# A six-layer local-attention transformer stage: clamp of the norms, layer norm's rows and the order of three steps changed

## The reference

```python
DIM, DEPTH, HEADS, DIM_HEAD, WINDOW = 128, 6, 16, 64, 32
DIM_INNER = int(DIM * 4 * 2 / 3)                         # 341
def l2norm(t):
    return t / jnp.maximum(jnp.linalg.norm(t, axis=-1, keepdims=True), 1e-12)
def attn_layer(x, Wqkv, qs, ksc, Wo):
    q, k, v = split of x @ Wqkv into 16 heads of 64
    q = rotary(l2norm(q) * qs); k = rotary(l2norm(k) * ksc)
    sim = q k^T * 8, masked to this and the previous window of 32
    return softmax(sim) v @ Wo
def ffn_layer(x, g, bln, W1, b1, W2, b2):
    mu = x.mean(-1, keepdims=True)
    var = ((x - mu) ** 2).mean(-1, keepdims=True)
    xn = (x - mu) / jnp.sqrt(var + 1e-05) * g + bln
    a, gate = jnp.split(xn @ W1 + b1, 2, -1)
    return a * jax.nn.gelu(gate, approximate=False) @ W2 + b2
for i in range(DEPTH):
    x = attn_layer(shift_tokens(x), ...) + x
    x = ffn_layer(shift_tokens(x), ...) + x
```

## Time and profile before

| | us |
|---|---|
| median of 3 runs | 6615.09 |
| lowest and highest | 6614.57, 6616.69 |
| the profiled execution's time | 6612.73 |
| its span on the core | 6610.9 |

### The profile page before, as it was taken

How to read it: one execution, slowest core, us unless ns; L and a number is a source line. 1 busy time by engine, 2 the same in 40 slices (tenths; PEclk the granted TensorE clock), 3 DMA queues, 4 the chain that set the end, 5 groups by cost and what they waited for, 6 DMA issues and landing times. The chain is left out here.

```text
span 6610.9 us, 172137 instructions
## 1 busy us (share of the span) xinstructions
PE 5118.0 (77%) x73958; PEld 3242.9 (49%) x74006; DVE 4022.1 (61%) x5250; ACT 3052.2 (46%) x4513; POOL 2655.6 (40%) x1366
## 2 busy tenths in 40 slices
PE   4749999999999999999999994888896444444446
PEld 3326666666666666666666662544543222122234
DVE  3167777777777777777877773233333544444554
ACT  1225555555555555555555552333333333343245
POOL 0025555555555555555555551111011444434400
PEclk9669999999999999999999996788887777777778
DMA  0010001001000100100010000000000000000000
GB/s 21 0 39 15 17 16 37 16 18 27 26 15 18 30 22 17 28 23 18 17 32 19 18 17 9 3 2 2 2 1 7 2 2 2 2 2 1 0 14 18
DMA packets 168396, 94.51 MB, mean 14 GB/s; under 512 B 122170, under 2 KB 155843, under 8 KB 167747
## 3 DMA queue, kind: packets, MB, share of 16 engines
q1 hardware_dynamic: 167747, 84.17, 4.6%
HBM read 23.75 MB, written 3.67 MB: 4 GB/s over the span
## 5 line engine op out<-in xcount | busy, mean ns | idle before, releaser
L930 POOL TENSOR_TENSOR tf_qk<-tf_qk,tf_rot 128x1024 f32<-128x1024 f32 x384 | 909.8, 2369 | 1425.5 <-DVE tf_rot L1299 1425.4
L985 PE MATMUL tf_psum<-tf_Wqkv,tf_xsT 128*128 128x512 f32 x1536 | 762.8, 620 | 116.6 <-issue 74.6
L1878 PE MATMUL mb_psum<-mb_read,ident 128*128 128x512 f32 x512 | 376.5, 883 | 604.3 <-POOL mb_read L1812 604.3
L937 POOL TENSOR_TENSOR tf_qk<-tf_qk,tf_rn 128x1024 f32<-128x1024 f32 x384 | 726.3, 1912 | 125.3 <-ACT tf_rn L1183 125.3
L1812 POOL TENSOR_TENSOR mb_read<-mb_state,mb_Csb 128x512 f32<-128x512 f32 x256 | 396.0, 1574 | 657.4 <-DVE mb_state L2029 644.5
L1176 ACT ACTIVATE tf_sq<-tf_psum 128x1024 f32<-128x1024 f32 x384 | 393.6, 1025 | 449.3 <-DVE tf_rot L1299 448.8
L1295 DVE TENSOR_TENSOR tf_qk<-tf_psum,tf_table 128x1024 f32<-128x1024 f32 x384 | 467.5, 1218 | 167.5 <-PE tf_psum L985 167.5
L1878 PEld LDWEIGHTS mb_psum<-mb_read,ident 128*128 128x128 f32 x512 | 130.4, 278 | 755.8 <-POOL mb_read L1812 636.8
L1058 PE MATMUL tf_psum<-tf_probT,tf_V 32*64 32x64 f32 (+1 forms) x27648 | 490.0, 219 | 4.4 <-issue 3.4
L985 PEld LDWEIGHTS tf_psum<-tf_Wqkv,tf_xsT 128*128 128x128 f32 x1536 | 271.0, 194 | 418.6 <-issue 408.5
L1299 DVE TENSOR_TENSOR tf_rot<-tf_psum,tf_table 128x1024 f32<-128x1024 f32 x384 | 466.2, 1214 | 0.0
(11 more groups left out here) (297 smaller groups left out, 9600.4 us busy)
## 6 DMA issues: line engine op xcount, KB each, us to landing
tf_zr<-z SPq DMA_DIRECT2D x96, 128.0 KB, 2.5
z<-tf_z SPq DMA_DIRECT2D x48, 256.0 KB, 3.0
tf_Wqkv<-in_Wqkv_split SPq DMA_DIRECT2D x18, 512.0 KB, 3.9
tf_zu<-z SPq DMA_DIRECT2D x97, 64.0 KB
tf_zu<-z SPq DMA_DIRECT2D x97, 63.5 KB
tf_zsh<-tf_z SPq DMA_DIRECT2D x96, 64.0 KB
tf_zsh<-tf_z SPq DMA_DIRECT2D x96, 63.5 KB
tf_Wo<-in_L_ffn_Wo SPq DMA_DIRECT2D x6, 512.0 KB, 3.9
```

The costliest lines, as they stand in the source:

```text
L930: nc.gpsimd.tensor_tensor(v, v, rot[:, kind, :], ALU.add).then_inc(added.sem, 1)
L937: nc.gpsimd.tensor_tensor(v, v, rn[:, t, HEADS * kind:HEADS * (kind + 1)].unsqueeze(2) .to_broadcast([P, HEADS, HD]), ALU.mult).then_inc(n ...
L985: last = nc.tensor.matmul(proj[:, half, :], xsT[:, step.unit(0), WIN + t * P:WIN + (t + 1) * P], Wqkv[:, c:c + 512], start=True, stop=True)
L1878: last = nc.tensor.matmul(y_ps[:, :], k.ident[:, :], read[:, m % 2, j, :, :], start=(m == 0 and j == 0), stop=(m == STEPS - 1 and j == 1), ...
```

## The change

Four edits of `transformer_stage`:

- `clamp` no longer reads a second tile. The sums of squares are stored at every other place of `ss`, the places between hold the constant 1e-24, and one `tensor_reduce` takes the maximum of each pair of places into a new tile `ssc`, which ScalarE's logarithm reads.
- The rows of layer norm go from VectorE (four `scalar_tensor_tensor` of 128x128, behind `clamp`) to GpSimd (`normalise_rows`: a subtraction and a multiplication of 128x512, between the two halves of `rope`), in the step with k % 4 = 0.
- In the step with k % 4 = 3, `widen(2)` goes behind `scores` on TensorE, `gelu(2)` behind the first `square` on ScalarE, `gate(2)` behind `centre` on VectorE. The load of the logarithm's table goes with `gelu(2)`.
- In the same step, `output` goes behind `project(step, 1)` on TensorE and `add_output` behind `rope(step, 1)` on VectorE.

```diff
@@ -715,7 +714,8 @@
         qk = sb("qk", [P, TT, 2, INNER])
         rot = sb("rot", [P, 2, INNER])
         sq = sb("sq", [P, 2, INNER])
-        ss = sb("ss", [P, TT, 2 * HEADS])
+        ss = sb("ss", [P, TT, 2 * HEADS, 2])
+        ssc = sb("ssc", [P, TT, 2 * HEADS])
         rn = sb("rn", [P, TT, 2 * HEADS])
         qT = sb("qT", [P, TT, PAIRS, P])
         kT = sb("kT", [P, PAIRS, WIN + T])
...
@@ -945,12 +945,23 @@
                 nc.gpsimd.tensor_tensor(v, v, rden[:, t, :, :].unsqueeze(3).to_broadcast([P, PAIRS, 2, HD]), ALU.mult)\
                     .then_inc(prob_ready.sem, 1)
 
+            def normalise_rows(J):
+                wide = lambda x: x.unsqueeze(2).to_broadcast([P, 4, P])
+                pool.wait_ge(ln_rstd.sem, ln_rstd.at(J, 1))
+                nc.gpsimd.tensor_tensor(xn[:, :, :], zsh[:, :, :], wide(moments[:, :, 0]), ALU.subtract)\
+                    .then_inc(xn_centred.sem, 1)
+                pool.wait_ge(xn_centred.sem, xn_centred.at(J, 1))
+                nc.gpsimd.tensor_tensor(xn[:, :, :], xn[:, :, :], wide(rstd[:, :]), ALU.mult).then_inc(xn_ready.sem, 1)
+
             def body(step):
                 if step.has(1):
                     normalise(step, 0)
                     normalise(step, 1)
                 if step.has(0):
                     rope(step, 0)
+                if step.k % 4 == 0 and step.has_pair():
+                    normalise_rows(step.pair())
+                if step.has(0):
                     rope(step, 1)
                 if step.has(2):
                     weigh(step)
@@ -1124,16 +1135,18 @@
                     project(step, 0)
                 if ff == 1:
                     turn_xn(step)
-                elif ff == 3:
-                    widen(step, 2)
                 if step.has(2):
                     scores(step)
+                if ff == 3:
+                    widen(step, 2)
                 if step.has(3):
                     turn_probs(step)
-                if step.has(4):
+                if step.has(4) and ff != 3:
                     output(step)
                 if step.has(0):
                     project(step, 1)
+                if step.has(4) and ff == 3:
+                    output(step)
                 if step.has(1):
                     turn_part(step, 0)
                 if step.has(3):
@@ -1178,7 +1191,7 @@
             def inverse_norm(step):
                 tau, t = step.tile(0), step.t(0)
                 act.wait_ge(clamped.sem, clamped.at(tau, 1))
-                nc.scalar.activation(rn[:, t, :], ss[:, t, :], ACT.Ln).then_inc(logged.sem, 1)
+                nc.scalar.activation(rn[:, t, :], ssc[:, t, :], ACT.Ln).then_inc(logged.sem, 1)
                 act.wait_ge(logged.sem, logged.at(tau, 1))
                 nc.scalar.activation(rn[:, t, :], rn[:, t, :], ACT.Exp, scale=-0.5).then_inc(rn_ready.sem, 1)
 
@@ -1230,9 +1243,7 @@
 
             def body(step):
                 ff = step.k % 4 if step.has_pair() else None
-                if ff == 3:
-                    gelu(step.pair(), 2)
-                if ff is not None and ff in (2, 3):
+                if ff == 2:
                     nc.scalar.preload_act_table_set('natural_log_exp_and_others')
                 if ff == 0:
                     inverse_deviation(step.pair())
@@ -1240,6 +1251,9 @@
                     copy_xn(step)
                 if step.has(0):
                     square(step, 0)
+                if ff == 3:
+                    gelu(step.pair(), 2)
+                    nc.scalar.preload_act_table_set('natural_log_exp_and_others')
                 if step.has(3):
                     copy_probs(step)
                 if step.has(2):
...
-            nc.vector.memset(least[:, :], 1e-24).then_inc(masks_ready, 1)
+            nc.vector.memset(ss[:, :, :, 1:2], 1e-24).then_inc(masks_ready, 1)
...
@@ -1302,14 +1316,14 @@
             def sum_squares(step, kind):
                 t = step.t(0)
                 dve.wait_ge(squared.sem, squared.at(step.tile(0), kind + 1))
-                nc.vector.tensor_reduce(ss[:, t, HEADS * kind:HEADS * (kind + 1)],
+                nc.vector.tensor_reduce(ss[:, t, HEADS * kind:HEADS * (kind + 1), 0],
                                         sq[:, kind, :].rearrange("p (h e) -> p h e", e=HD), AX.X, ALU.add)\
                     .then_inc(summed.sem, 1)
 
             def clamp(step):
                 tau, t = step.tile(0), step.t(0)
                 dve.wait_ge(summed.sem, summed.at(tau, 2))
-                nc.vector.tensor_tensor(ss[:, t, :], ss[:, t, :], least[:, :], ALU.max).then_inc(clamped.sem, 1)
+                nc.vector.tensor_reduce(ssc[:, t, :], ss[:, t, :, :], AX.X, ALU.max).then_inc(clamped.sem, 1)
 
             def centre(step):
                 tau, t = step.tile(2), step.t(2)
@@ -1351,14 +1365,6 @@
                     last = nc.vector.bn_aggr(moments[:, s, :], stats[:, s, :])
                 last.then_inc(ln_moments.sem, 1)
 
-            def normalise(J):
-                dve.wait_ge(ln_rstd.sem, ln_rstd.at(J, 1))
-                for s in range(4):
-                    last = nc.vector.scalar_tensor_tensor(out=xn[:, s, :], in0=zsh[:, s, :], scalar=moments[:, s, 0:1],
-                                                          in1=rstd[:, s:s + 1].to_broadcast([P, P]), op0=ALU.subtract,
-                                                          op1=ALU.mult)
-                last.then_inc(xn_ready.sem, 1)
-
             def gate(J, j):
                 m = FF_BLOCKS[j][1]
                 dve.wait_ge(hidden.sem, hidden.at(J, j + 1))
@@ -1378,23 +1384,23 @@
                     statistics(step.pair())
                 if step.has(0):
                     rope(step, 0)
+                if step.has(2):
+                    centre(step)
                 if ff == 3:
                     gate(step.pair(), 2)
-                if step.has(2):
-                    centre(step)
-                if step.has(4):
+                if step.has(4) and ff != 3:
                     add_output(step)
                 if step.has(0):
                     sum_squares(step, 0)
                     rope(step, 1)
+                if step.has(4) and ff == 3:
+                    add_output(step)
                 if step.has(2):
                     denominator(step)
                 if step.has(0):
                     sum_squares(step, 1)
                     clamp(step)
-                if ff == 0:
-                    normalise(step.pair())
-                elif ff == 1:
+                if ff == 1:
                     gate(step.pair(), 0)
                 elif ff == 2:
                     gate(step.pair(), 1)
```

More of the change, by code:

```diff
@@ L703, in transformer_stage @@
         eps = sb("eps", [P, 1])
-        least = sb("least", [P, 2 * HEADS])
         base = sb("base", [P, 4, TT, HD])
@@ L763, in transformer_stage @@
             ev(n) for n in "scored maxed centred exped den_sum den_inv prob_ready o_copied out_done z_added".split())
-        ln_stats, ln_moments, ln_logged, ln_rstd, xn_ready = (
-            ev(n) for n in "ln_stats ln_moments ln_logged ln_rstd xn_ready".split())
+        ln_stats, ln_moments, ln_logged, ln_rstd, xn_centred, xn_ready = (
+            ev(n) for n in "ln_stats ln_moments ln_logged ln_rstd xn_centred xn_ready".split())
         hidden, gelued, gated, y_done, y_added = ev("hidden", 3), ev("gelued", 3), ev("gated", 3), ev("y_done"), ev("y_added")
@@ L916, in _ @@
         def _(pool):
-            for e in (added, normed, prob_ready):
+            for e in (added, normed, prob_ready, xn_centred, xn_ready):
                 e.start(pool)
@@ L1272, in _ @@
             for e in (roped, summed, clamped, maxed, centred, den_sum, den_inv, z_added, ln_stats, ln_moments,
-                      xn_ready, gated, y_added):
+                      gated, y_added):
                 e.start(dve)
```

## The result

The changed kernel takes 6456.98 us in the median of 4 runs (6445.00 to 6467.24), the kernel before 6614.83 us in 4 runs beside it (6608.31 to 6616.69). The ratio is 0.9762, with a 95% interval of 0.9744 to 0.9781: 158 us faster. Forecast were 6481 in a range of 6455 to 6540, so the time lies in the range, near its low end. The profiled execution took 6459.57 us, 153 less than that of before, where the sum of the prediction said 134 less.

What follows compares the result with a forecast made beforehand. TensorE's queue was taken as the bound. Gains of 73 + 38 + 60 = 171 us less 37 (22, 5 and 10) gave 134 net: 6612.7 to 6479, as a median 6481 us, range 6455 to 6540 (8 in 10).

Steps and rivals of the forecast that it cites:

- the three waits: TensorE's once-per-pair waits for `tf_xn` (65.8 us), `tf_hT` (53.9) and `tf_xsT` (30.2), claimed to go, but for the last round.
- (b): Rival: the clamp's reduction is blocked as well, lasting as long as `weigh` (1.84 us); 6557 us, chance 0.06.
- (d): Rival: GpSimd becomes the bound, needing its two row operations to take over 10 us together; chance next to nothing.
- (a): Rival: another wait takes more back, by `add_output` 1.3 us late (6522) or doubled unreleased waits (6546); chance 0.18.
- Rival (c): Slower: TensorE's instruction feed bounds the stage, so gains return as unreleased waits; 6685 us, chance 0.04.
- The rows, 73 us: Layer norm's rows on GpSimd end TensorE's wait for `tf_xn`: 1.56 us a pair, 73 us gained.
- The clamp, 38 us: Earlier inverse norms let the input's copy end before `widen(0)` does: 0.8 us a pair, 38 us gained.
- `widen(2)` behind the scores, 60 us: In the step k % 4 = 3, `widen(2)` no longer waits for its gate: 1.26 us x48, 60 us gained.
- The new wait, 22 us: Zeroing of `mixed` waits for `add_output`, now behind k's rotation: 0.4 to 0.5 us x48, 22 us lost.
- The changes of layer, 5 us: At five changes of layer q's weights come later through SyncE's queue: 0 to 2 us each, 5 us lost.
- The allowance for unreleased waits, +10: TensorE's waits that nothing in the profile releases ("issue") may grow by 0 to 74.6 us; 10 us taken as lost.

Runs made afterwards that it cites:

- e3: Kernel before with only the new order of the step k % 4 = 3 on the three engines: 6610.04 us, ratio 1.0006.
- e5: Changed kernel with the old clamp, tensor_tensor against `least`: 6540.43 us, ratio 0.9893.
- e2: Kernel before with only layer norm's rows moved to GpSimd (`normalise_rows`): 6540.57 us, ratio 0.9898.
- e4: Changed kernel with layer norm's rows back on VectorE behind `clamp`: 6633.85 us, ratio 1.0044.
- e1: Kernel before with only the clamp as a reduction and the `ss` layout it needs: 6617.43 us, ratio 1.0018.
- e7: Changed kernel with the old order of the step k % 4 = 3, so clamp and rows only: 6440.64 us, ratio 0.9745.
- e8: Changed kernel with the clamp as a one-input tensor_scalar maximum with an immediate: 6534.81 us, ratio 0.9889.

## Why the prediction was right, and where it wasn't

**The mechanism of each wait: right.** The reduction escapes `weigh` (0.22 us, forecast 0.2 to 0.25), the rows take 2.1 us on GpSimd (1.04 each, forecast 2.1 with the wait), the three waits went and the fourth came at the size that was forecast: 17.5 us idle, and 11.23 - 10.74 = 0.49 us a pair by starts, 24 us against 22. Rivals (b) and (d) are out by these rows, and (a), which needed `add_output` 1.3 us late or the unreleased waits doubled. Rival (c) is out as well: the waits that nothing in the profile releases did not take the gains, the largest row is 68.7 us where it was 74.6.

**Why the reduction escapes: right in the outcome, thin in the reasons.** The prediction took one input in SBUF as the reason, and the `tensor_scalar` with one input was held all the same (1.83 us). Its other evidence, the two reductions of the earlier trace rows, doesn't carry it either: GpSimd's sum ended at 2149.06, ahead of the first, and the next began at 2152.67, behind the start of the second. A third one in the kernel before does, since it begins inside GpSimd's sum and is no longer for it:

```profile
2152.67 2.38 POOL L930 TENSOR_TENSOR tf_qk<-tf_qk,tf_rot 128x1024 f32<-128x1024 f32 x1 [3.61 <-DVE tf_rot L1299]
...
2153.92 1.16 DVE L1305 TENSOR_REDUCE tf_ss<-tf_sq 128x16 f32<-128x1024 f32 x1
```

**The rows, 73 us: right.** Alone they bring 67. But the clamp's worth depends on them: without them on GpSimd, or at an earlier place, its 1.6 us are worth nothing. The prediction took the wait for `tf_xn` as the rows' matter and never asked what the new clamp does to operations that stand right behind it, though the gap that they used stands in the earlier trace rows: 125.3 us that GpSimd waits for the inverse norms in front of L937. It didn't need to for the sum of all parts, since the rows had left that place. It would have needed to for any part of it.

**The clamp, 38 us: mis-sized.** The term counted only the input's copy, with 0.77 us a pair measured (2.49 - 1.72). The same earlier inverse norms bring the gate of `widen(1)` forward, which is worth 0.84 us a pair in the step k = 7. The prediction says so itself ("the clamp alone brings it to about 1.5"), and then books the whole wait, 60 us, to the next step. With the old order still in place the clamp and the rows bring 164 us; the clamp's share in that surrounding is 164 - 67 = 97. Against the rows alone, `tf_xsT` falls by 28.9 us (30.0 to 1.1), `tf_hT` by 37.0 (58.8 to 21.8) and the rows without a releaser by 23.9 (122.6 to 98.7), 90 us of idle time together. The 46 restarts that go with `tf_xsT` are some 7 more (an estimate, 0.16 each, from 1.26 against 1.10); the waits for `tf_hT` are shorter but as many, 49.

**`widen(2)` behind the scores, 60 us: wrong as the worth of the order.** What the clamp leaves for it is 21.8 - 4.9 = 16.9 us idle, some 24 with the 46 restarts. Against that stand the 24 of the new wait and the layer changes. The order changes the time by +2 us alone, -3 beside the rows and +4 beside both, all within the intervals; beside the clamp alone it costs 16, about half of it by the seven more drops of the clock.

**The sum: two errors against each other.** By the runs it reads 67 for the rows, 97 for the clamp and -4 for the order, 160 us. The prediction had 73, 38 and 33 (60 - 22 - 5), less 10 for growth: 134. Much of this cancels by necessity, since the wait for `tf_hT` goes only once and the prediction booked it to the order instead of the clamp. The rest does not: the unreleased waits fell where 10 us of growth were booked, and the measured gains (153 to 160 us) came 19 to 26 above the sum. That this still lay inside the range is in part luck, for single terms were off by 37 and 59 us.

**The new wait, 22 us: right, and avoidable.** One operation's place decides it: `add_output` between the rotation's halves gets 15 us back, where the prediction took k's rotation as one piece.

**The changes of layer, 5 us: too small.** With 0 to 2 us for each of the five I took 1. The waits ahead of q's projection show 14.1 us more than with the old order (96.6 against 82.5), and 9.4 in the later profile of the changed kernel (91.9). The other pairs of kernels that differ in the order alone show 8.9 (e3), 10.9 (e5 against e2) and 12.0 (e4 against e1), so some 2 to 3 us each. The counts and the releaser speak for the queue in which the wait for `z_added` stands ahead of the weights. No experiment loads the weights earlier, so this is read from waits and not shown by a run of its own.

**The allowance for unreleased waits, +10: wrong in its sign.** The rows of the stage without a releaser sum to 117.8 us before and 111.2 after, in a window over the whole stage, and the prediction had only the largest of them in view. The decrease and the 10 together are some 16 of the 19 us by which the profiled execution beat the sum. Most of the decrease stands ahead of the turns. This is the row before, whose counterpart with clamp and rows alone (e7) stands above at 8.4:

```profile
PE tf_psum L967 <- issue: 23.4, 23, 1.5
```

It goes with the clamp: 22.7 to 28.0 us in the five kernels whose clamp is held by `weigh` (before, e2, e3, e5, e8), 4.5 to 11.5 in the nine with the reduction. By what way the clamp shortens it stays open. The sum was 98.9 us in the later profile of the changed kernel; the kernel before was 10 us faster in that batch as well, so this doesn't explain the 12 us between the two medians.

**The slower kernels.** Nothing in the prediction allowed for a part of the change that is slower by itself, and two combinations were, by 9 and 26 us. The rule that VectorE waits for GpSimd was used for the instruction that goes, and not for those that its going would let start inside GpSimd's work. That a longer wait would also bring TensorE's lower clock was in no term either.

## What to carry to other kernels

Before an instruction is shortened because it is stalled, look at what comes behind it on its engine and on the engine that stalls it: the successor starts where the stall was and inherits it, and the other engine may lose the very pause in which the successor ran (here 2.77 us became 5.88). A wait that grows can cost more than its own length, when TensorE's clock falls behind it (some 1.2 us here, behind a wait of 2.77). Terms that act on one wait can't be added as parts: work out what is left of the wait after the first edit, and price the second from there. The short two-input VectorE operations here cost nothing extra in GpSimd's pauses (0.34 us) and one GpSimd instruction each inside a run of them (1.8 to 2.0 us), so their place counted for more than the engine they ran on. A short maximum against a constant can be written as a reduction over pairs, which ran beside GpSimd in 0.22 us where the other two forms took 1.8.

## What the runs showed of the hardware

- A run of short two-input VectorE operations beside back-to-back GpSimd ones alternates with them: in the timeline shown, four operations that take 1.13 us free take 5.88, one GpSimd instruction of 1.9 us for each of the first three (1802, 1982 and 1983 ns), and 339 ns for the last, once GpSimd stands still.
- A one-input `tensor_scalar` on floats from SBUF to SBUF is blocked as well (181 ns free, 1824 in the median), a `tensor_reduce` over twice the elements isn't (219 to 223 in all 192).
- Behind a wait of 2.76 to 2.78 us TensorE was granted 0.50 to 0.69 of its clock over the next 4 us in 29 of 46 cases (clamp alone) and in 36 of 46 (e4), and all of it in the others. Behind waits of 1.28 to 1.30 us at the same place (before) it kept all of it in 46 of 46.
- GpSimd's 128x512 operation with a broadcast takes 1.04 us whether it subtracts or multiplies. The rows need two of them, 2.1 us, where VectorE's four fused operations take 1.13 us in all.
